# Routed attention: tokens fetched by indirect DMA instead of gathered by one-hot matmuls

## The reference

```python
q_top, q_idx = top_k(einsum('bnd,gd->bgn', x, w_qr), NQ)
kv_top, kv_idx = top_k(einsum('bnd,gd->bgn', x, w_kvr), NK)
queries, key_values = x[bidx, q_idx], x[bidx, kv_idx]      # rows of x
q = queries @ w_q.T;  k, v = split(key_values @ w_kv.T)    # per route
v = v * sigmoid(kv_top)
k, v = [null_k, k], [null_v, v]                            # one more key
o = softmax(q k^T * DH**-0.5) v @ w_out.T * sigmoid(q_top)
summed = zeros.at[q_idx].add(o);  counts = zeros.at[q_idx].add(1)
out = where(counts > 0, summed / clip(counts, 1e-5), null_token)
```

## Time and profile before

| what | us |
|---|---|
| median of 3 runs | 3162.34 |
| the runs | 3149.78 to 3163.03 |
| the profiled execution | 3159.7 |
| its span in the profile | 3158.0 |
| TensorE busy in the span | 2790.3 (88%) |
| VectorE busy | 1952.1 (62%) |
| ScalarE busy | 1404.1 (44%) |
| GpSimd busy | 1036.9 (33%) |

### The profile page before, as it was taken

How to read it: one execution, slowest core, us unless ns; L and a number is a source line. 1 busy time by engine, 2 the same in 40 slices (tenths; PEclk the granted TensorE clock), 3 DMA queues, 4 the chain that set the end, 5 groups by cost and what they waited for, 6 DMA issues and landing times. The chain is left out here.

```text
span 3158.0 us, 62333 instructions
## 1 busy us (share of the span) xinstructions
PE 2790.3 (88%) x24321; PEld 1829.7 (58%) x24352; DVE 1952.1 (62%) x4335; ACT 1404.1 (44%) x2960; POOL 1036.9 (33%) x1448
## 2 busy tenths in 40 slices
PE   6999799988799968887888799997999989799997
PEld 2343477756577756565556567764666556456664
DVE  7989555556555576634773566665667646466664
ACT  5655144434244435322553354443555534355553
POOL 4878223223223222312112333330222246212222
PEclk9899799999899989879999899999999999999999
DMA  2000100011000001100101000002222201112221
GB/s 79 1 1 1 54 2 1 2 25 28 1 1 2 1 1 48 66 27 20 29 22 31 15 1 1 1 4 72 67 70 70 70 18 32 59 42 73 81 67 46
DMA packets 54256, 97.07 MB, mean 31 GB/s; under 512 B 6042, under 2 KB 40870, under 8 KB 53200
## 3 DMA queue, kind: packets, MB, share of 16 engines
q1 hardware_dynamic: 52688, 92.49, 9.4%
q0 software_dynamic: 1280, 0.60, 0.1%
HBM read 71.76 MB, written 21.76 MB: 30 GB/s over the span
## 5 line engine op out<-in xcount | busy, mean ns | idle before, releaser
L566 ACT ACTIVATE s_sT<-s_R 128x1024 f32<-128x1024 f32 (+2 forms) x448 | 400.3, 946 | 199.5 <-PE s_R L500 198.6
L601 DVE TENSOR_REDUCE s_negm<-s_R 128x4 f32<-128x1024 f32 x320 | 377.2, 1221 | 153.6 <-PE s_R L471 153.5
L471 PE MATMUL s_R<-s_qk 32*128 32x256 f32 (+2 forms) x3584 | 241.8, 383 | 58.0 <-ACT s_sT L566 33.1
L500 PE MATMUL s_R<-s_qA,s_qk 32*128 32x256 f32 (+2 forms) x3584 | 240.7, 382 | 18.3 <-DVE s_negm L601 11.7
L573 ACT ACTIVATE s_oc<-s_OB 128x256 f32<-128x256 f32 x224 | 85.8, 383 | 338.3 <-PE s_OB L519 338.3
L519 PE MATMUL s_OB<-s_sT,s_v 128*32 128x256 f32 (+2 forms) x3584 | 224.1, 368 | 9.9 <-ACT s_sT L566 6.4
L471 PEld LDWEIGHTS s_R<-s_qk 32*128 32x128 f32 x3584 | 153.9, 185 | 106.1 <-issue 79.6
L616 DVE TENSOR_TENSOR s_qA<-s_qk,s_X 128x256 f32<-128x256 f32 x224 | 94.4, 421 | 194.7 <-PE s_X L531 194.7
L500 PEld LDWEIGHTS s_R<-s_qA,s_qk 32*128 32x128 f32 x3584 | 162.4, 184 | 79.2 <-issue 65.1
L1511 POOL TENSOR_TENSOR s_pr<-s_pr,s_rinv 128x1024 f32<-128x1024 f32 x64 | 121.1, 1893 | 219.6 <-DVE s_rinv L1621 219.6
L1593 ACT ACTIVATE s_pr<-s_S,s_negmax 128x256 f32<-128x256 f32 x256 | 118.5, 470 | 135.5 <-DVE s_negmax L1624 135.5
(11 more groups left out here) (585 smaller groups left out, 6307.9 us busy)
## 6 DMA issues: line engine op xcount, KB each, us to landing
s_wB<-enc_b SPq DMA_DIRECT2D x32, 962.5 KB, 4.8
s_scratch<-s_pk SPq DMA_DIRECT2D x58, 256.0 KB, 2.0
s_qk<-s_scratch SPq DMA_DIRECT2D x232, 64.0 KB
s_wA<-enc_a SPq DMA_DIRECT2D x32, 193.0 KB, 5.0
big<-moe SPq DMA_DIRECT2D x2, 2347.0 KB, 11.0
big<-routed SPq DMA_DIRECT2D x2, 2084.0 KB
all_W<-weights SPq DMA_DIRECT2D x1, 2182.0 KB, 15.5
all_W<-weights SPq DMA_DIRECT2D x1, 2181.5 KB, 10.7
```

Of the source, the lines that this page charges most:

```text
L471: last = pe.matmul(S[h][:, t * T:t * T + hi - lo], b.qk[rows, r % 2, 0, c, t * P:(t + 1) * P], b.qk[rows, r % 2, 1, c, lo:hi], start=(t == ...
L500: last = pe.matmul(b.R[:, a.turned_at(u, h // 2), :][:, h % 2, a.at(kt)], b.qk[rows, r % 2, 1, c, kt * P:(kt + 1) * P], b.qA[rows, u % 2, ...
L566: act.activation(b.sT[:, u % (a.lag + 1), 2 * p:2 * p + 2, 0:a.width], b.R[:, a.turned_at(u, p), 0:a.width], ACT.Exp).then_inc(s.expd, 1)
L601: ins = dve.tensor_reduce(b.negm[:, u % 2, :, at].rearrange("p t h -> p h t"), S.rearrange("p h (t k) -> p h t k", t=TT), AX_X, ALU.max, n ...
```

## The change

What TensorE did by one-hot matrices is done by GpSimd's indirect DMA, which reads rows of a tensor in HBM at positions that stand in `index`.

- SyncE stores the normed `h` to a tensor `sent` in HBM while the search runs.
- The search keeps all 128 found values in `best` and adds `dve.max_index` to each round, which notes their positions in `found`; `work` has two halves in turn. The running sum and the slot numbers are gone. The positions go back to partitions as `place` and, with the batch's first row added, as `index`. The sigmoids are taken of the found values only. Counts per token come from a small product of the mask on TensorE.
- `fetch(u)` issues two indirect DMAs for unit u, of 128 query rows and 64 key rows, into a ring of eight units. GpSimd issues units 0 to 7 at the start of the stage and unit i+8 after it has divided the weights of unit i.
- The `gather` piece is now the transposes of the fetched rows, 384 columns for two units instead of 512. The values are scaled by ScalarE as it evicts them.
- The `turn` has only the transpose of `pn`. The scatter matrix `sqT` is written by VectorE in `place_rows(i)`: one instruction compares the token numbers with the unit's positions and multiplies with its sigmoids. Its four buffers are reused, so it waits for the scatter of unit i-4.

```diff
@@ routed_attention_stage, the search @@
                     for k in range(NQ // 8):
-                        d.done(dve.max(best[:], work[:]))
-                        d.done(dve.match_replace(out=work[:], in_to_replace=best[:], in_values=work[:],
-                                                 imm_value=NEG))
-                        if 8 * (k + 1) == NK:
-                            d.done(dve.tensor_tensor(mask_kv[:], work[:], row[:], ALU.not_equal))
-                    d.done(dve.tensor_tensor(mask[:], work[:], row[:], ALU.not_equal))
...
-                    d.done(dve.tensor_tensor_scan(out=csum[:], data0=ones_row[:], data1=mask[:], initial=0.0,
-                                                  op0=ALU.mult, op1=ALU.add))
...
+                        eight = slice(8 * k, 8 * k + 8)
+                        d.done(dve.max(best[:, eight], work[:, k % 2, :]))
+                        d.mark(dve.match_replace(out=work[:, 1 - k % 2, :], in_to_replace=best[:, eight],
+                                                 in_values=work[:, k % 2, :], imm_value=NEG))
+                        d.done(dve.max_index(found[:, eight], best[:, eight], work[:, k % 2, :]))
...
+                    dve.wait_ge(sig_ready, 1)
+                    d.done(dve.tensor_copy(place[:], ST[:, 0:ROWS]))
+                    d.mark(dve.tensor_tensor(index[:], place[:], g.w("r_first"), ALU.add))
@@ TensorE, the front pieces and the turn @@
-                                pe.wait_ge(scaled, group * NB + bb + 1)
-                                for h in range(TT):
-                                    last = pe.matmul(f[:, (bb % 2) * 256:(bb % 2 + 1) * 256], g.h[:, TT * b + h, :],
-                                                     oh[:, bb, h, :], start=(h == 0), stop=(h == TT - 1))
+                                u = group * NB + bb
+                                at, ring = (bb % 2) * (NQ + NK), u % (2 * NB)
+                                pe.wait_ge(got_q[ring], 16 * (u // (2 * NB) + 1))
+                                pe.transpose(f[:, at:at + NQ], hq[:, ring, :], g.ident[:])
+                                pe.wait_ge(got_k[ring], 16 * (u // (2 * NB) + 1))
+                                last = pe.transpose(f[:, at + NQ:at + NQ + NK], hk[:, ring, :],
+                                                    g.ident[0:NK, 0:NK])
...
-                            for h in range(TT):
-                                pe.transpose(f[:, h * P:(h + 1) * P], sq[:, j % (2 * NB), h, :], g.ident[:])
-                            last = pe.transpose(f[0:H, 2 * P:3 * P], pn[:, j % 2, :], g.ident[:])
+                            last = pe.transpose(f[0:H, 0:P], pn[:, j % 2, :], g.ident[:])
@@ GpSimd @@
+                        if u >= 2 * NB:
+                            before = u - 2 * NB
+                            pool.wait_ge(f_mm, plan.number[("gather", before // NB, before % NB // 2)] + 1)
+                        pool.indirect_dma_start(hq[:, ring, :], None, sent,
+                                                bass.IndirectOffsetOnAxis(index[:, q:q + 1], 0),
+                                                bounds_check=NTOK - 1, oob_is_err=False).then_inc(got_q[ring], 16)
...
+                    for u in range(NB):
+                        fetch(u)
+                    null_keys(0)
+                    for u in range(NB, 2 * NB):
+                        fetch(u)
...
+                        if i + 2 * NB < U:
+                            fetch(i + 2 * NB)
@@ VectorE @@
-                    make_onehots(0)
+                    def place_rows(u):
+
+                        c = columns(u)[0]
+                        if u >= 4:
+                            dve.wait_ge(scattered, u - 3)
+                        dve.tensor_scalar(sqT[:, u % 4, :], g.iota_free[:], place[:, c:c + 1], sig[:, 0, c:c + 1],
+                                          ALU.is_equal, ALU.mult).then_inc(placed, 1)
...
-                            if i % NB == 0 and i // NB + 1 < plan.GROUPS:
-                                make_onehots(i // NB + 1)
+                            place_rows(i)
                             dve.wait_ge(expd, i + 1)
```

More of the change, by code:

```diff
@@ L2973, in routed_attention_stage, with _ @@
             NW = sr.ps("NW", [P, 512])
-            loaded, turned, hT_cp, nw_mm = [sr.sem(n) for n in ("loaded", "h_turned", "hT_cp", "nw_mm")]
-            logits, lg_ready, rows_ready, slots_ready, back, steps = [
-                sr.sem(n) for n in ("logits", "lg_ready", "rows_ready", "slots_ready", "back", "steps")]
-            with nc.Block() as block:
-                if big is not None:
-                    which, iota = big
-                    @block.sync
-                    def _(sp):
+            loaded, turned, hT_cp, nw_mm, sig_ready = [
+                sr.sem(n) for n in ("loaded", "h_turned", "hT_cp", "nw_mm", "sig_ready")]
+            logits, lg_ready, rows_ready, sorted_, mask_ready, back, counted, steps, stored = [
+                sr.sem(n) for n in ("logits", "lg_ready", "rows_ready", "sorted", "mask_ready", "back", "counted",
+                                    "steps", "stored")]
+            with nc.Block() as block:
+                @block.sync
+                def _(sp):
+                    in_rows = sent.rearrange("(t p) d -> p t d", p=P)
+                    if have:
+                        sp.dma_start(in_rows[:, 0:TT * have, :], g.h[:, 0:TT * have, :]).then_inc(stored, 16)
+                    if big is not None:
+                        which, iota = big
                         width = g.big_n[which]
@@ L2986, in _ @@
                         sp.dma_start(g.BIG[:, half:width], g.a[which][:, half:width]).then_inc(loaded, 16)
+                    sp.wait_ge(ln.h_ready, B - have)
+                    sp.dma_start(in_rows[:, TT * have:, :], g.h[:, TT * have:, :]).then_inc(stored, 16)
+                    sp.wait_ge(stored, 32 if have else 16)
+                    if big is not None:
                         sp.wait_ge(loaded, 32)
@@ L3024, in _ @@
                     last.then_inc(nw_mm, 1)
-                    pe.wait_ge(steps, 27)
+                    pe.wait_ge(steps, 35)
                     keep_busy(pe, g, HT[:, 0, :], 16)
-                    pe.wait_ge(slots_ready, 1)
+                    pe.wait_ge(sorted_, 3)
+                    pe.transpose(ST[:, 0:ROWS], found_f[:], g.ident[0:ROWS, 0:ROWS])
+                    pe.transpose(ST[:, ROWS:2 * ROWS], best[:], g.ident[0:ROWS, 0:ROWS])
+                    last = pe.transpose(ST[:, 2 * ROWS:3 * ROWS], best_kv[:].rearrange("r k n -> r (k n)"),
+                                        g.ident[0:ROWS, 0:ROWS])
+                    last.then_inc(back, 1)
+                    pe.wait_ge(mask_ready, 1)
                     for h in range(TT):
-                        last = pe.transpose(ST[:, h * ROWS:(h + 1) * ROWS], csum[:, h * P:(h + 1) * P],
-                                            g.ident[0:ROWS, 0:ROWS])
-                    last.then_inc(back, 1)
+                        last = pe.matmul(LT[:, h * B:(h + 1) * B], mask[:, h * P:(h + 1) * P], g.w("r_perbatch"),
+                                         start=True, stop=True)
+                    last.then_inc(counted, 1)
                     keep_busy(pe, g, HT[:, 0, :], 8)
@@ new lines, in _ @@
+                    dve.tensor_tensor(mask[:], work[:, 0, :], row[:], ALU.not_equal).then_inc(mask_ready, 1)
+                    dve.wait_ge(sig_ready, 1)
+                    d.done(dve.tensor_copy(place[:], ST[:, 0:ROWS]))
+                    d.mark(dve.tensor_tensor(index[:], place[:], g.w("r_first"), ALU.add))
+                    dve.wait_ge(counted, 1)
+                    of = LT[:, 0:TT * B].rearrange("p (h b) -> p h b", h=TT)
+                    d.done(dve.tensor_copy(count[:], of))
@@ L3105, in routed_attention_stage, with columns @@
             left = {U - B + 5 + r: r for r in range(leave)}
-            (onehots, scaled, nullk, f_mm, f_cp, scored, maxed, shifted, expd, summed, recip, normed, turned,
+            (placed, nullk, f_mm, f_cp, scored, maxed, shifted, expd, summed, recip, normed, turned,
              prT_cp, pv, oT_cp, projected, o_cp, scattered, added, nulled) = [
-                sa.sem(n) for n in ("onehots", "scaled", "nullk", "f_mm", "f_cp", "scored", "maxed", "shifted",
+                sa.sem(n) for n in ("placed", "nullk", "f_mm", "f_cp", "scored", "maxed", "shifted",
                                     "expd", "summed", "recip", "normed", "turned", "prT_cp", "pv", "oT_cp",
                                     "projected", "o_cp", "scattered", "added", "nulled")]
+            got_q = [sa.sem(f"got_q{k}") for k in range(2 * NB)]
+            got_k = [sa.sem(f"got_k{k}") for k in range(2 * NB)]
+            def columns(u):
+                s, b = plan.unit(u)
+                return b * 2 * G + s, b * 2 * G + G + s
             def copied(*item):
```

98 lines of the change are left out of this document (40 added, 58 removed).

## The result

The changed kernel takes 3189.89 us (median of 4 runs, 3183.12 to 3193.25) against 3162.69 before: ratio 1.0092, interval 1.0065 to 1.0119. It is slower by nearly 1%, where I had forecast no change, and outside my range. The profiled execution has a span of 3181.4 us, 23.4 more than before. Counted from its first instruction to the first of the next layer, the first routed layer takes 13.0 us more (316.91 for 303.89) and the second 11.3 (311.32 for 300.02); the rest of the program gives back 0.9. I expected -1.0 each. The profiled execution was the shortest of the four, and the medians differ by 27.2 us: a fall of the clock at the loop's end, which other executions show (under "Filler at the start"), is not in these 23.4.

A forecast was written before the change was run, and what follows sets the result against it. TensorE bound the unit loop, and after the change a circle of waits through VectorE would. -12.1 + 4.8 + 5.3 + 1.0 = -1.0 us a stage, -2 us for two, gave 3159 us; 8-in-10 range 3132 to 3182.

The forecast's parts named there:

- search: Search before the attention stage: position search added to each round, shorter tail; +4.8 us a stage (+3.7 to +7.2).
- first fetch to first projection: Attention stage's start: the first projection waits for eight indirect DMAs, 12.4 us instead of 7.1, so +5.3.
- -12.1: Unit loop: sum of all step changes and the shorter first gather, in us a stage.
- gather steps: Unit-loop steps that also gather the next group: from 9.20 to 6.67 us each (-2.53).
- plain ones: Unit-loop steps without gather or q or k projections: from 5.70 up to 6.67 us each (+0.97).
- The circle through `place_rows`: Unit loop: VectorE's wait for unit i-4's scatter closes a circle of waits once per unit, 6.67 us (6.57 to 6.71).
- q and k steps: Unit-loop steps with q or k projections: TensorE work exceeds the wait chain, so each just loses 0.28 us.
- my third rival: GpSimd's issuing is held up beside VectorE: at 3 us per DMA, steps of 7.9 us, 3199 us; chance 0.07.
- My first rival: Unit loop: VectorE gets past its wait sooner, TensorE is fed in time; -27 a stage, 3129 us; chance 0.14.
- I charge +1.0: Attention stage's start: TensorE idles, then returns at a lower clock, partly during projections; +1.0 us a stage (-1 to +4).
- My second rival: TensorE's clock falls: a tenth of the 220 us loop at 1.2 GHz adds 11 us a stage, 3181 us; chance 0.17.
- The price of eight transposes: Gather in the unit loop: eight transposes of fetched rows at 1.04 us replace 16 matmul rows of 3.72 us.

The follow-up runs named there:

- Filler at the start: The changed kernel with 55 instead of 5 filler matmuls on TensorE at the start of each attention stage; ratio 1.0089 to the kernel before.
- plain fetches: The changed kernel with SyncE's plain DMAs of fixed rows in place of GpSimd's indirect DMAs, output not the reference's; ratio 1.0027 to the kernel before.

## Why the prediction was wrong

The steps, in a stage (first layer; the sums are of spans):

| term of the prediction | forecast | measured |
|---|---|---|
| search | +4.8 | +3.7 |
| search's end to first fetch | 0 | +1.3 |
| first fetch to first projection | +5.3 | +5.7 |
| first projection to first scatter, clock included | -3.7 | +1.4 |
| first to last scatter | -7.4 | -4.2 |
| end of the stage | 0 | +5.1 |
| sum | -1.0 | +13.0 |

(My -12.1 and +1.0 are the fourth and fifth line together: -7.4 is the part of -12.1 from the first scatter on, six gather steps, six q, six k, nine plain ones and the last.)

**Right.** The circle through `place_rows`: 6.59 us for 6.67 forecast, the new instruction 0.41 for 0.44, its remedy worth what the steps say (13.05 us measured, 9 x 1.17 + 2.4 = 13). q and k steps lose 0.26. The search and the start of the attention, from the first fetch on: in their bounds. GpSimd's issues are hidden in the loop and took 0.94 to 1.29 us, never 3: my third rival was wrong. The 3100 ns that the Trainium skill gives for a DMA beside a two-port VectorE operation ("SBUF — State Buffer", on the two separate sides) did not come in this kernel, neither in the loop nor beside the search's rounds; whether any VectorE instruction there is of that kind, no row shows. My first rival's sum was also wrong: its own terms (six gather steps at -2.96, 25 others at -0.28, the first gather at -3.9) give -28.7 a stage, not -27.

**Wrong, in order of size.**

(1) The stage's end had no term in the sum: I took it to cost what it did. GpSimd's closing of a stage in which it has issued 64 indirect DMAs takes 5 us more, 0.08 us each, and here GpSimd is among the last to finish, so all wait. The expert layer, my source for indirect DMAs, did not show it: its last one starts at 1472.62 and VectorE's additions go on until 1480.92, so a closing of a few us lies under them.

(2) The step "I charge +1.0" for the clock. The stretch took 5.1 us more than forecast, and by an estimate nearly 3 of these are the clock. By the stretches shown the clock is low for 16.6 us (the share missing to 1.00, doubled, times each length); before, the 12 us from 385 to 397 at 0.72 made 6.7, which is 3.4 us lost. At 1.00 all through the stretch took 32.8 us in the place of 38.9, so the low clock now costs some 6. My sum left 3.2: the 3.4, less 1.2 for the shorter gather at half speed (1.9 in its 5.59, 0.7 in my 1.7), plus 1.0. The rest, some 2.2 us, is that the stretch gains less at full clock than I took. It was 37.4 less 3.4, that is 34.0; my terms take 3.5 off (0.84, and 3.72 less 1.04), but 32.8 came, not 30.5. At full clock the shorter gather uncovers the waits of 0.83 us for `pn` and 0.90 us for VectorE; before, behind the products of 5.59 us, the trace has neither. My second rival had the clock, but placed its fall in the loop.

(3) The price of eight transposes, 1.04 by the earlier trace rows, was for one shape in a run; with shapes in turn it is 1.84. I also took off the 16 products' duration, 3.72, where the distance to the next start was 3.56 (481.80 to 485.36). In my sum the circle (6.67) bound a gather step; in truth TensorE's own work does (7.27): 0.6 x 6 = 3.6 us, 3.2 in the table since the plain steps came 0.07 shorter than forecast.

(4) The hand-over of 1.3 us to the first fetch had no term; its cause was not looked for.

Open: the runs show that GpSimd's closing goes by the number of indirect DMAs, not why. Nor is it settled what makes the clock fall in some executions at the end of the loop; each time TensorE had waited in plain steps just before, and where the circle was removed no profile had it.

## What to carry to other kernels

When a ring buffer's reuse wait is put into an in-order queue, put it behind an instruction that waits for the same event already; ahead of the chain that feeds the next step it closes a circle (13 us a stage here). Here a ring of eight buffers or the later place in the queue each took it away. When work goes to indirect DMAs, count them at the end of the stage too, and let the engine that issued them finish early; and fetch what is known early while another engine still searches. When work leaves TensorE, ask what its waits do to the clock, and price transposes with their neighbours' shapes.

## Hardware behaviour not expected

Each indirect DMA of a stage adds about 0.08 us between GpSimd's last instruction of the stage and the next stage: 1.81 us before the change with none, 4.30 with 32, 6.20 with 56, 6.91 with 64. (The plain fetches, also with none, left 2.26, so the first 32 may cost less.) Filling TensorE's waits gave back up to 6.1 us of one stretch. With the start filled, the low spell of the projections goes and one after the first scores stays; with the waits at the scores filled, it is the other way round, and a short one comes later. A transpose costs 0.13 us in a run of its shape and 0.20 to 0.26 next to another shape.
